# Eight-wide attentions of a six-layer decoder: the second half of the heads divided by their sums straight from PSUM

## The reference

```python
def _L0_xattn_ref(x_q, x_kv, w_q, w_kv, w_proj, w_rel):        # r1
    q, (k, v) = x_q @ w_q, split(x_kv @ w_kv)
    logits = einsum('bhqd,bhkd->bhqk', q, k) * SCALE + rel * w_rel
    attn = softmax(logits)
    out = einsum('bhqk,bhkd->bhqd', attn, v)
    return out.transpose(0, 2, 1, 3).reshape(B, Tq, 128) @ w_proj

def _L1_attn_ref(X, Wq, Wk, Wv, Wo, bo):                       # r2
    S_ = where(causal, -inf, Q @ K.T)
    Z = softmax(S_ / sqrt(8)) @ V
    return Z.reshape(b, n, 128) @ Wo.T + bo

x = _layernorm(x + _L0_attn_ref(x, ...))           # landmark attention, six Newton steps
x = _layernorm(x + _L0_xattn_ref(x, ctx_1024, ...))
x = _layernorm(x + _L0_ffn_ref(x, ...))            # eight experts, one chosen
x = _layernorm(x + _L1_attn_ref(x, ...))
x = _layernorm(x + _L1_xattn_ref(x, ctx, ctx, mask, ...))  # 16 heads of width 64
x = _layernorm(x + _L1_ffn_ref(x, ...))
```

## Time and profile before

| | us |
|---|---|
| three timed runs | 2509.76, 2513.37, 2516.99 |
| median | 2513.37 |
| span of the profiled execution, first to last instruction | 2520.2 |
| TensorE busy | 2266.3 (90%) |
| VectorE busy | 1956.9 (78%) |
| ScalarE busy | 1450.1 (58%) |
| GpSimd busy | 387.1 (15%) |
| chain that ended last, by engine | PE 52%, DVE 28%, ACT 15% |

### The profile page before, as it was taken

One profiled execution on the slowest core, in us unless ns is written; L12 is line 12 of the kernel. 1 busy time (PEld: TensorE's weight loads), 2 busy tenths in 40 slices (PEclk: granted clock), 3 DMA queues, 4 the chain that ended last, 5 costly groups with the idle time before them and its releaser, 6 DMA issues.

```text
span 2520.2 us, 95538 instructions
## 1 busy us (share of the span) xinstructions
PE 2266.3 (90%) x40576; PEld 1846.1 (73%) x40576; DVE 1956.9 (78%) x6166; ACT 1450.1 (58%) x5093; POOL 387.1 (15%) x530
## 2 busy tenths in 40 slices
PE   6789999999999999999999999999999999999875
PEld 3677777777777777777777777777777777777764
DVE  3568888888888888788888888788888888888652
ACT  3346666656656655656656565665656566566531
POOL 2101111111111111111111111111111111111110
PEclk9889999999999999999999999999999999999885
DMA  4200000000000000000000000000000000000000
GB/s 192 90 7 9 5 7 9 9 9 9 9 5 7 9 9 8 9 5 8 8 9 9 9 9 5 8 8 9 9 9 9 5 7 9 9 9 8 6 3 2
DMA packets 29960, 35.75 MB, mean 14 GB/s; under 512 B 3544, under 2 KB 28128, under 8 KB 28384
## 3 DMA queue, kind: packets, MB, share of 16 engines
q1 hardware_dynamic: 29536, 29.65, 3.4%
HBM read 27.54 MB, written 2.10 MB: 12 GB/s over the span
## 4 chain that ended last, share of the span: by engine, by line
PE 52%; DVE 28%; ACT 15%; issue 4%; POOL 0%; DMA 0%; SPq 0%; POOLq 0%; DVEq 0%; ACTq 0%
PE ps L477 29%; PE ps L480 8%; ACT probs L1062 5%; PE ps L744 4%; DVE probsT L1349 3%; PE ps L828 3%; ACT probs L1047 3%; PE ps L876 2%; ACT ey L985 2%; DVE x_rows L1211 2%; DVE small L1252 2%; PE ps L761 2%; PE ps L665 2%; DVE qk_v L1337 1%; DVE p L1254 1%
## 5 line engine op out<-in xcount | busy, mean ns | idle before, releaser
L1102 POOL TENSOR_TENSOR small<-small,weights 128x1 f32<-128x1 f32 x256 | 149.0, 582 | 1142.7 <-DVE small L1200 1142.7
L1010 ACT ACTIVATE probs<-ps,small 128x128 f32<-128x128 f32 x1024 | 286.1, 384 | 31.0 <-DVE small L1342 29.5
L1349 DVE COPY probsT<-ps 128x512 f32<-128x512 f32 x384 | 263.1, 685 | 36.3 <-PE ps L480 32.7
L480 PE MATMUL ps<-weights,probs 128*128 128x128 f32 x1536 | 256.1, 292 | 32.8 <-ACT probs L1010 15.4
L1342 DVE TENSOR_REDUCE small<-ps 128x4 f32<-128x512 f32 x384 | 254.2, 683 | 20.5 <-PE ps L828 10.7
L1113 POOL TENSOR_TENSOR probs<-probs,small 128x256 f32<-128x256 f32 x128 | 108.7, 849 | 885.6 <-DVE small L1478 885.6
L480 PEld LDWEIGHTS ps<-weights,probs 128*128 128x128 f32 x1536 | 178.7, 146 | 86.3 <-ACT probs L1010 44.6
L929 ACT COPY x_T<-ps 128x128 f32<-128x128 f32 x128 | 34.1, 267 | 302.9 <-PE ps L480 302.9
L1062 ACT ACTIVATE probs<-ps,small 128x128 f32<-128x128 f32 x512 | 181.6, 375 | 20.5 <-DVE small L1342 19.0
L477 PE MATMUL ps<-wz,ss 64*64 64x72 f32 x6144 | 157.4, 229 | 32.5 <-DVE wz L1294 32.4
L1293 DVE SCALAR_TENSOR_TENSOR wz<-ey,ss 128x256 f32<-128x256 f32 x320 | 142.0, 444 | 51.1 <-ACT ss L970 36.9
(11 more groups left out here) (199 smaller groups left out, 5400.0 us busy)
## 6 DMA issues: line engine op xcount, KB each, us to landing
weights<-in_wpack SPq DMA_DIRECT2D x3, 1759.0 KB
fc_A<-in_b SPq DMA_DIRECT2D x2, 2048.0 KB, 14.3
fc_A<-in_a SPq DMA_DIRECT2D x2, 2048.0 KB, 11.4
x_in_T<-in_xT SPq DMA_DIRECT2D x32, 64.0 KB, 1.8
x_in_rows<-in_x SPq DMA_DIRECT2D x32, 64.0 KB, 1.8
ctx_T<-in_ctxT SPq DMA_DIRECT2D x32, 64.0 KB, 1.9
ctx_rows<-in_ctx SPq DMA_DIRECT2D x32, 64.0 KB, 1.9
mask_i<-in_mask SPq DMA_DIRECT2D x32, 64.0 KB, 1.9
```

Of the source, the lines that this page charges most:

```text
L480: return nc.tensor.transpose(dst, src, ident)
L1010: ins = nc.scalar.activation(probs(s, g)[:, j], bank(s, SCORE_BANK[g], 128 * j, 128), ACT.Exp, bias=sm(s, "nb", 4 * g + j, 1), scale=-1.0)
L1102: nc.gpsimd.tensor_tensor(sm(s, out), sm(s, ve), w("mhalf"), ALU.pow).then_inc(sem(done, s), 1)
L1349: V.tensor_copy(probsT(s, n % 4).rearrange("p a b -> p (a b)"), bank(s, 2)).then_inc(sem("pT", s), 1)
```

## The change

ScalarE's second copy (`evict(1)`, steps `r1.o1` and `r2.o1`) is dropped, and `o_rows` holds 8 heads. VectorE's step `rows`, at the same place in its list, now runs two pairs instead of one: reciprocal and multiplication of the first 8 heads from `o_rows`, then, after a wait for TensorE's last values (`pv`), of the other 8 straight from bank 1 of PSUM. TensorE waits for both (`z` counts 2 for each attention). The turned context of r1 goes to bank 0 instead of bank 1, without the wait for a copy. The Nystrom part has the same instructions as before.

```diff
@@ PLACES, "act" @@
-r1.e0 98.871  r1.e1 98.981  r1.o0 101.434  r1.e2 103.400  r1.e3 108.646  r1.o1 113.872  r1.z 117.267
+r1.e0 98.871  r1.e1 98.981  r1.o0 101.434  r1.e2 103.400  r1.e3 108.646  r1.z 117.267
...
-r2.o0 158.943  r2.e2 168.611  r2.e3 168.907  r2.o1 172.082  r2.z 172.083
+r2.o0 158.943  r2.e2 168.611  r2.e3 168.907  r2.z 172.083
@@ build @@
-        orow = lane("o_rows", [128, H, HD + 1])
+        orow = lane("o_rows", [128, H // 2, HD + 1])
@@ TensorE @@
         def tail_zT(s, n):
-            pe.wait_ge(sem("z", s), at("z", s, n))
+            pe.wait_ge(sem("z", s), at("z", s, n if s == NYS else 2 * n))
...
-                    pe.wait_ge(sem("o_rows", s), at("o_rows", s, n_o + 1))
+                    pe.wait_ge(sem("o_rows", s), at("o_rows", s, n_att))
...
             if n_att == 1:
-                pe.wait_ge(sem("o_rows", s), at("o_rows", s, 2))
                 pe.wait_ge(sem("y_norm", s), at("y_norm", s, 1))
-                turned(bank(s, 1, 0, 128), cn[s][:]).then_inc(sem("y_nT_ps", s), 1)
+                turned(bank(s, 0, 0, 128), cn[s][:]).then_inc(sem("y_nT_ps", s), 1)
@@ ScalarE @@
-            def evict(pair):
-                act.wait_ge(sem("pv", s), at("pv", s, n_e + 2 * pair + 2))
-                copy(orow[s][:, 8 * pair:8 * pair + 8].rearrange("p h e -> p (h e)"), bank(s, pair, 0, 72)).then_inc(sem("o_rows", s), 1)
+            def evict():
+                act.wait_ge(sem("pv", s), at("pv", s, n_e + 2))
+                copy(orow[s][:].rearrange("p h e -> p (h e)"), bank(s, 0, 0, 72)).then_inc(sem("o_rows", s), 1)
...
-            evict(1)
-            yield f"{a}.o1"
@@ VectorE @@
+        def by_sums(s, v, a):
+
+            n = v.shape[1]
+            link(V.reciprocal(sm(s, "rs", a, n), v[:, :, HD]))
+            V.tensor_tensor(z[s][:, a:a + n], v[:, :, 0:HD], over(sm(s, "rs", a, n), HD), ALU.mult).then_inc(sem("z", s), 1)
+
-        def tail(s, n):
-            if s == NYS:
-                dve.wait_ge(sem("o_ps", s), at("o_ps", s, 1))
-                v = bank(s, 1, 0, H * (HD + 1)).rearrange("p (h e) -> p h e", e=HD + 1)
+        def tail(s, n, pair):
+            if pair == 0:
+                dve.wait_ge(sem("o_rows", s), at("o_rows", s, n))
+                by_sums(s, orow[s][:], 0)
             else:
-                dve.wait_ge(sem("o_rows", s), at("o_rows", s, 2 * n))
-                v = orow[s][:]
-            link(V.reciprocal(sm(s, "rs"), v[:, :, HD]))
-            V.tensor_tensor(z[s][:], v[:, :, 0:HD], over(sm(s, "rs"), HD), ALU.mult).then_inc(sem("z", s), 1)
+                dve.wait_ge(sem("pv", s), at("pv", s, 4 * n))
+                by_sums(s, bank(s, 1, 0, 72).rearrange("p (h e) -> p h e", e=HD + 1), H // 2)
...
-            tail(s, n_att)
+            tail(s, n_att, 0)
+            tail(s, n_att, 1)
             yield f"{a}.rows"
             if n_att == 1:
-                V.tensor_scalar(cnT[s][:], bank(s, 1, 0, 128), w("y_g"), w("y_b"), ALU.mult, ALU.add).then_inc(sem("y_norm", s), 1)
+                V.tensor_scalar(cnT[s][:], bank(s, 0, 0, 128), w("y_g"), w("y_b"), ALU.mult, ALU.add).then_inc(sem("y_norm", s), 1)
```

More of the change, by code:

```diff
@@ L178 @@
     "ln_T_ps": 4, "ln_rows": 5, "ln_rstd": 6, "ln_ve": 6, "m_gate": 2, "m_gate_act": 2, "m_gate_ps": 2, "m_h0": 2,
-    "m_h1": 2, "m_h_ps": 4, "m_nT": 1, "m_y": 4, "nb": 12, "o_rows": 4, "pT": 12, "pT_ps": 12, "proj": 6, "pv": 12,
+    "m_h1": 2, "m_h_ps": 4, "m_nT": 1, "m_y": 4, "nb": 12, "o_rows": 2, "pT": 12, "pT_ps": 12, "proj": 6, "pv": 12,
     "s_ps": 12, "sub": 4, "xT": 4, "xbo": 2, "y_crstd": 1, "y_cve": 1, "y_mask": 1, "y_nT_ps": 2, "y_norm": 4,
-    "y_o8": 2, "y_p": 8, "y_proj_ps": 6, "y_qk": 4, "y_rs": 4, "y_v8": 2, "z": 2, "zT": 2, "zT_ps": 2,
+    "y_o8": 2, "y_p": 8, "y_proj_ps": 6, "y_qk": 4, "y_rs": 4, "y_v8": 2, "z": 4, "zT": 2, "zT_ps": 2,
 }
@@ L648, in attention8 @@
             yield f"{a}.proj"
-            n_e, n_o, n_p = 4 * (n_att - 1), 2 * (n_att - 1), 4 * (n_att - 1)
+            n_e, n_p = 4 * (n_att - 1), 4 * (n_att - 1)
             def scores(pair):
@@ L1020, in attention8 @@
                 yield f"{a}.e{g}"
-            evict(0)
+            evict()
             yield f"{a}.o0"
@@ L1315, in nystrom @@
             yield "n.w"
-            tail(s, 1)
+            dve.wait_ge(sem("o_ps", s), at("o_ps", s, 1))
+            by_sums(s, bank(s, 1, 0, H * (HD + 1)).rearrange("p (h e) -> p h e", e=HD + 1), 0)
             yield "n.rows"
```

## The result

| | before | after |
|---|---|---|
| median of the timed runs, us | 2515.18 | 2551.68 |
| lowest to highest | 2509.76 to 2528.64 (4) | 2545.52 to 2555.76 (4) |
| span of the profiled execution | 2520.2 | 2550.8 |

The ratio is 1.0138, interval 1.0104 to 1.0171. The direction was forecast, the size was not: 36.5 us instead of 11.6, and 2551.68 lies above the range. The launch that was profiled after the change took 2552.83 us, 2 us more than its span.

What follows compares the result with a forecast made beforehand. The prediction took no single engine as the bound, but the chain of work handed between engines. Terms of 9.9 (r1), 2.1 (r2) and -0.4 (last tail) gave +11.6 us, from 2513.37 to 2525.0 us, range 2515 to 2535.

Steps and rivals of the forecast that it cites:

- The r1 pair: VectorE's added pair in the r1 tail: z ends 0.32 us later in 31 tails, +9.9 us.
- a shared port: Bound for the r1 tail: VectorE and GpSimd split the port's bandwidth, z 0.22 us later, 6.8 us.
- The r2 pair: VectorE's added pair in the r2 tail: z 0.28 us later, its turn 0.07 us later, 30 times, +2.1 us.
- The dropped copy: ScalarE's 64 dropped copies of 0.22 us: none on the path in the steady state, 0 but for the last tail.
- Rivals B and C: B: a later wait swallows the delay, 2514 us, chance 0.12; C: ScalarE bound behind the r1 tail, 2506 us, chance 0.05.
- The turned context: r1's turned context in bank 0: one wait less, no reader that waits for it, 0 us.
- Rival A: More idle in TensorE's r1 tail brings more stretches at half clock, 10 us more, 2535 us, chance 0.15.

Runs made afterwards that it cites:

- split_only: Kernel before with two VectorE pairs instead of one in both eight-wide tails, both from `o_rows`, copies and waits kept: 2531.75 us, ratio 1.0063.
- r2_only: Kernel before with the change in the r2 attention alone, r1 left as before: 2517.84 us, ratio 0.9988.
- after_pad: Changed kernel with one already satisfied TensorE wait put back ahead of r1's turned context, 2561 instructions a batch: 2536.76 us, ratio 1.0059.
- ctx0: Kernel before with only r1's turned context moved to bank 0, without its wait for `o_rows`: 2520.37 us, ratio 0.9981.
- after_shift: Changed kernel with satisfied TensorE waits, 16 instructions, added once at the start; still 2560 a batch: 2539.32 us, ratio 1.0055.
- after_pad_ln2: Changed kernel with the satisfied wait ahead of the second layer norm's turn instead, 2561 instructions a batch: 2541.53 us, ratio 1.0068.

## Why the prediction was right in direction and wrong in size

**The r1 pair (+9.9): right.** Every step came as written: first multiplication 0.09 us behind GpSimd (0.08), the second 0.55 us after the first one's start and 0.23 long, z 0.31 later (0.32). The exclusive lock that the Trainium skill, "SBUF — State Buffer", "SBUF: two separate sides", states agrees with the trace: half the numbers took as long (0.41 us) as all had (0.42), and the tail grew by 0.31, not by the 0.22 of a shared port. split_only shows that the two pairs alone do it. One row was misread without harm: the 0.22 us of the earlier trace rows, taken for a multiplication without such a neighbour, is of one from PSUM; from SBUF and without the neighbour it takes 0.22 to 0.23 as well.

**The r2 pair (+2.1): not contradicted.** TensorE doesn't wait, VectorE's cover went from 0.56 to 0.38. r2_only can't be told from zero.

**Together**, the period at full clock went from 72.72 to 73.07 in after_pad, in which only the border has been moved away. 29 x 0.35 = 10.2 us, where the prediction has 9.9 + 2.1 for the whole. By the ratio after_pad lost 15 us (10 to 19), where the forecast is 11.6. That its span of 2532.3 all but hits the forecast 2531.8 is luck: its executions went from 2530 to 2539. So is the 73.20 of the changed kernel: the forecast had started from one period of 72.80 and not from the mean of 72.72, and some 0.1 of the 73.20 is the border.

**The dropped copy (0): right.** ScalarE's wait for the turned z grew from 0.29 to 0.69, and split_only, which keeps the copy, is as fast as after_pad. Rivals B and C fell: TensorE's wait and the period grew.

**The turned context (0): this step failed.** The text said "one wait less and no reader that waits for it". Both are true, and ctx0, which has this step alone, lost nothing that can be measured. But the wait is also an instruction of TensorE. With it gone the batch has 2560 instructions instead of 2561, and the border of a program piece lies in a dense burst in every batch. In the changed kernel the term that was put at 0 costs 10 to 21 us; why so much there and so little in ctx0, no run shows. I looked at what waits and never at how long the list is; the row that could have told me, the queue of 321 instruction transfers, was on the page.

How that price divides is partly open. By the full-clock period it is 0.10 us (73.17 against 73.07, but from 2 periods), by the `ey` matmuls 0.36: 7.5 us more of busy and 3.9 of idle time over 32 batches (148.6 and 26.6 against 141.1 and 22.7). That is 3 to 10 us. The rest of the 21.7 us between after_pad's 29 periods and the changed kernel's goes with 13 more falls of the clock, at 1.0 to 1.4 each by the rows of the kernel before. Why the stall draws falls, no run shows; they also vary between executions of kernels that time the same (23, 33 and 30 falls in after_pad, after_shift and after_pad_ln2).

**Rival A: its mechanism was right, its worth was not.** The falls behind the tail (10 in these 29 periods before; the prediction had counted 9) went to 17 in split_only and 18 in after_pad, with 0.3 to 0.4 us more waiting there. They cost 1.4 us each (72.72 against 74.09; I had taken 1.0 from another kind). But in after_pad the other falls went from 16 to 5, and the balance is nil: 10.8 us over the 29 periods, of which 10.2 are the longer path. The Trainium skill, "TensorE: Matmul & The Clock Gate", "What's actually happening", lets the gate follow recent activity; the filled waits agree, with no fall left behind the tail, yet a count of falls in one place didn't give the time.

**The range** of 2515 to 2535 fits the kernel without the border (1.0059 of 2513.37 is 2528) and misses the changed one by 17 us. The working had a bound for each duration and none for an effect of the list itself.

## What to carry to other kernels

Before an edit adds or drops instructions on an engine with a long unrolled list, count its instructions for one period and compare with the size of its program pieces: an exact multiple fixes the border at one place, and if that is a dense burst, try a satisfied wait more. Here it gave 0.3 to 0.8% of the time in the three pairs that differ by it. Measure it rather than count on it: ctx0 had the stalls and lost nothing that can be measured. Splitting an operation so that a half can start early pays only if the half is also put earlier in its engine's list; behind the same neighbour it is a longer path. Where VectorE works beside GpSimd, put the part with an operand in PSUM there, and the part with two SBUF inputs elsewhere.

## What the runs showed of the hardware

- TensorE's instructions come in pieces of 256 (321 transfers for 82272, 325 for 1024 more), and at the border of a piece a dense burst of small matmuls stalls by up to 0.49 us. In the kernel before, where the border wanders, no burst shows it.
- A VectorE multiplication with one input in PSUM wasn't held by GpSimd: 0.23 us under its operation, in 31 tails, against 0.41 for the same size with both inputs in SBUF.
- Unread matmuls in TensorE's wait removed every fall of the clock behind it, from 24 to 0 and from 10 to 0, and no kernel gained: falls came elsewhere, 18 to 24 in all, and the period at full clock grew by 0.2 to 0.6 us.
